# Second attention: each roll's two keys in rows of their own, and one transpose per tile and half

## The chip, the cores and the metric

One core of a Trainium2 chip runs the whole program. The metric is the device time in microseconds, from 3 runs of the kernel before; the profile is of one further execution. The engines are PE (TensorE; its weight loads are listed as PEld), DVE (VectorE), ACT (ScalarE), POOL (GpSimd) and SP (the queue that issues the DMAs). An engine works through its own queue in order.

## What is computed

The input is x of 16 sequences of 256 tokens with 128 features. Four blocks follow one another, each on a layer norm of x and added to x: a causal attention with 16 heads of 64, a slot FFN, a second attention, and the slot FFN again. The second attention is what matters here:

```python
N, S, D = x.shape; H = 16; hd = D // H            # 16, 256, 128; hd = 8
q = (x @ Wq.T).reshape(N, S, H, hd).transpose(0, 2, 1, 3)
k = (x @ Wk.T).reshape(N, S, H, hd).transpose(0, 2, 1, 3)
v = (x @ Wv.T).reshape(N, S, H, hd).transpose(0, 2, 1, 3)
att = jnp.einsum('nqhd,nkhd->nhqk', q, k)         # q and k run over the 16 heads
att = jax.nn.softmax(att / jnp.sqrt(jnp.asarray(hd, x.dtype)), axis=3)
out = jnp.einsum('nhqk,nkhd->nqhd', att, v).reshape(N, S, D)
return out @ Wo.T + bo
```

After the transpose the second axis is the head, so for every token there are 16 x 16 scores between the heads of that same token, a softmax over them, and a weighted sum of the token's 16 value vectors. The last reshape mixes tokens and heads, which the kernel does by a round trip through DRAM.

## The kernel before

**Order.** The four blocks run one after the other. The second attention works through 16 batches, one sequence of 256 tokens (QT = 2 tiles of 128) each. b_steps writes out by hand the order of the steps of one batch; two batches (par 0 and 1) make one trip of a loop, and run_plan gives the same list to every engine, which picks the steps that concern it. While batch b does its softmax and weighting, the same list holds the rolls, dot products and flips of batch b + 1, and the norm, xt and qk of batch b + 2. "v", "turn", "xt", "qk", "yt" and "project" take turns in two PSUM banks R.

**Scores of one batch.** Queries and keys lie with the feature (head, element) on the 128 partitions and the token along the row: b_qt in f32, the keys as a high and a low f16 part, b_kh and b_kl. For each shift n of 0 to 15 the key of head (h + n) mod 16 is needed beside the query of head h. A "roll" step j does two shifts, 2j and 2j + 1: PE multiplies a permutation matrix by the keys (lines 695 and 697, four f16 matmuls of 256 columns) into one of two banks T (T[j % 2]), after the product two rolls ago has read that bank, and DVE multiplies it by the queries (line 811) into b_prod. There are 8 rolls, 0 to 7. After rolls 0 to 3 comes "dots" 0, after 4 to 7 "dots" 1: four f32 matmuls (line 704) sum the 8 elements of each head by the 0/1 matrix heads; that of roll 4j + n writes partitions 32n to 32n + 15 of bank M[j] (heads has 32 columns, of which the last 16 are zero), 512 columns wide: 256 tokens of the roll's first shift, then 256 of its second. ACT copies the bank to b_st (line 770). "flip" j then turns tokens onto the partitions: per tile t and shift parity e one f32 matmul (line 713) with 128 tokens of b_st as the stationary operand and 64 picked columns of the identity as the moving one, into O, the scores laid out as (tile, shift, head).

**What follows.** "soft": DVE takes the row maximum (line 817, waits for both flips), "shift": PE subtracts it in the bank (line 686), ACT takes the exponential (line 773), DVE sums and inverts it (820, 822). "weigh" 0 and 1: POOL multiplies values and exponentials (line 858), "gather" 0 and 1: DVE sums these over the shifts (line 826). "normal": POOL divides (847), SP stores b_o to DRAM and loads b_y back (1225, 1230); "yt" and "project": PE transposes b_y (722) and applies the output matrix (727 to 736); "add": ACT (780). For the batch ahead: "norm" on DVE and POOL (356, 360, 364, 365), "apply" on ACT (759), "xt": PE transposes (670), ACT and DVE split into xh and xl (751, 800), "qk": PE, then ACT and DVE make b_kh, b_kl and b_qt (753, 803, 755).

**Order on PE within one batch**: v, early (roll 0), shift, roll 1, yt, roll 2, project, roll 3, roll 4, dots 0, roll 5, roll 6, flip 0, roll 7, xt, dots 1, qk, flip 1. On DVE: soft, norm, products 0 and 1, gather 1, products 2 and 3, sumexp, products 4, 5, 6 and 7, xl, gather 0, b_kl.

Of the kernel before, what the change touches and what calls it, by code (L numbers as in the profile page):

```python
# [22 lines left out]
ACT = mybir.ActivationFunctionType  # L23
# [3 lines left out]
NB, SEQ, D = 16, 256, 128  # L27
NT = NB * SEQ // 128
QT = SEQ // 128
H = 16  # L30
# [196 lines left out]
def build(nc, x_in, w_in, shapes, scratch, out):  # L227
    ctx = ExitStack()
    with ctx:
# [85 lines left out]
        b_qt = sb("b_qt", [128, 2, SEQ])  # L315
        b_kh, b_kl = sb("b_kh", [128, 2, SEQ], F16), sb("b_kl", [128, 2, SEQ], F16)
        b_prod = sb("b_prod", [128, ROLLS, 2, SEQ])
        b_st = sb("b_st", [128, 2, 2 * SEQ])
        b_v = sb("b_v", [128, 2, QT, EB, 2 * H])
        b_e = sb("b_e", [128, 2, QT, H, H])  # L320
        b_nm, b_rs = sb("b_nm", [128, QT, H], BF16), sb("b_rs", [128, 2, QT, H])
# [336 lines left out]
        def b_tensor(pe):  # L658
            def do(step, i, fill):
# [40 lines left out]
                elif kind == "dots":  # L700
                    pe.wait_ge(b_multiplied, ROLLS * (b + 1) + 4 * j + 4)
                    wait(pe, b_raised, 2 * b + j + 1)
                    for n in range(4):
                        ins = pe.matmul(M[j][32 * n:32 * n + 32, :], w["heads"][:, :],  # L704
                                        b_prod[:, 4 * j + n, :, :].rearrange("p e t -> p (e t)"), start=True, stop=True)
                    ins.then_inc(b_dotted, 1)
                elif kind == "flip":
                    pe.wait_ge(b_raised, 2 * (b + 1) + j + 1)
                    if j == 0:
                        wait(pe, b_exped, b)  # L710
                    for t in range(QT):
                        for e in range(2):
                            ins = pe.matmul(O[nx][:, t * 256 + 128 * j:t * 256 + 128 * j + 128]  # L713
                                            .rearrange("p (n e h) -> p n e h", n=4, e=2)[:, :, e, :],
                                            b_st[:, j, e * SEQ + t * 128:e * SEQ + t * 128 + 128],
                                            ident[:, :].rearrange("p (n h) -> p n h", n=4)[:, :, 0:H],
                                            start=j == 0 and t == 0 and e == 0, stop=False, skip_group_check=True)
                    ins.then_inc(b_flipped, 1)
                elif kind == "yt":
                    pe.wait_ge(b_loaded, 16 * (b - 1))  # L720
# [20 lines left out]
        def b_scalar(act):  # L741
            bank = [None]

            def do(step, i, fill):
# [17 lines left out]
                elif kind == "v":  # L762
                    wait(act, b_weighed, 2 * b)
                    for n in range(2):
                        ins = act.activation(b_v[:, 1 - par, :, :, n * H:(n + 1) * H],
                                             src[:, 0:SEQ].rearrange("p (t h e) -> p t e h", t=QT, h=H), ACT.Copy)
                    ins.then_inc(b_values, 1)
                elif kind == "dots":
                    act.wait_ge(b_dotted, 2 * (b + 1) + j + 1)
                    act.activation(b_st[:, j, :], M[j][:, :], ACT.Copy).then_inc(b_raised, 1)  # L770
                elif kind == "shift":
                    act.wait_ge(b_shifted, b + 1)
                    act.activation(b_e[:, par, :, :, :], O[par][:, :].rearrange("p (t s h) -> p t h s", t=QT, s=H),  # L773
                                   ACT.Exp, scale=EB ** -0.5).then_inc(b_exped, 1)
                elif kind == "project":
                    bank[0] = R[fill.bank], fill.count
                elif kind == "add":
                    projected, count = bank[0]
                    act.wait_ge(b_filled, count)
                    act.activation(X[:, bass.ds((b - 2) * QT, QT), :], projected[:, 0:SEQ]  # L780
                                   .rearrange("p (t d) -> p t d", t=QT), ACT.Copy).then_inc(b_added, 1)
                elif kind == "yt":
                    act.activation(b_yt[:, :], src[:, 0:SEQ], ACT.Copy).then_inc(b_turned, 1)
# [512 lines left out]
def constants():  # L1296
# [9 lines left out]
    for n in range(H):  # L1306
        for h in range(H):
            for e in range(EB):
                roll[EB * ((h + n) % H) + e, n, EB * h + e] = 1.0
    heads = np.repeat(np.eye(H, 32, dtype=np.float32), EB, axis=0)  # L1310
    onehot = np.zeros((128, 2, 128), np.float32)
    for pair in range(2):
        onehot[[pair, 64 + pair], pair, :] = 1.0
# [65 lines left out]
```

## Time and profile before

| | before |
|---|---|
| runs, median (lowest to highest) | 974.3 us (974.05 to 974.79) |
| profiled execution | 972.47 us |
| its span, first to last instruction | 970.7 us |
| mean granted TensorE clock | 0.929 |
| busy: PE / DVE / ACT / POOL | 82% / 70% / 49% / 42% of the span |
| second attention | from about 631 to 872 us of the span |

Times within the trace are us from the start of the span. Busy times are sums over instructions; a matmul's time is that from its start to its modelled end, so neighbouring matmuls overlap and their busy times don't add up to time in the queue. "x8" is the number of instructions merged into a row, and the time is then that from the start of the first to the end of the last. In brackets stands how long the engine was idle before, and whose end released it.

### The profile page before, as it was taken

To read this page: it belongs to the slowest core of one execution; us is meant where nothing else is said; L and a number is where in the kernel's file an instruction comes from. 1 tells how busy PE (TensorE), PEld (TensorE's weight loads), DVE (VectorE), ACT (ScalarE), POOL (GpSimd) and SP (SyncE) were. 2 spreads that over 40 slices of the span, in tenths; PEclk is the share of its full clock that TensorE was granted. 3 is DMA by queue.
4 is the path that set the end of the run, shared out by engine and by line. 5 is a ranking of instruction groups with operands and counts; after the bars stand their busy time and mean duration, and the time that the engine had idled before them with its cause. 6 is when DMAs were issued, how large, how long until landed. Compare 5 with 4: busy or idle time off the path is not lost.

```text
span 970.7 us, 25469 instructions
## 1 busy us (share of the span) xinstructions
PE 799.1 (82%) x10228; PEld 614.3 (63%) x10228; DVE 682.4 (70%) x1560; ACT 472.6 (49%) x801; POOL 408.9 (42%) x302
## 2 busy tenths in 40 slices
PE   2899999999999999999995876668888888839655
PEld 1687777877788777877774453534555555525434
DVE  4677666676666766676664776548999999967763
ACT  1667666676666766776661423023333433315220
POOL 1445444444455444454442100018877778851000
PEclk9999999999999999999997977679999999957786
DMA  6000000000000000000000000000111111120002
GB/s 264 2 3 1 0 0 0 0 0 0 0 0 0 0 0 0 0 0 0 1 2 2 1 0 1 1 1 11 17 18 20 22 22 18 20 27 1 1 1 87
DMA packets 71586, 13.17 MB, mean 14 GB/s; under 512 B 66432, under 2 KB 70528, under 8 KB 70912
## 3 DMA queue, kind: packets, MB, share of 16 engines
q1 hardware_dynamic: 71552, 12.71, 6.0%
q8 instruction: 23, 0.38, 0.2%
q14 instruction: 11, 0.09, 0.0%
HBM read 8.51 MB, written 4.19 MB: 13 GB/s over the span
## 4 chain that ended last, share of the span: by engine, by line
PE 67%; DVE 19%; issue 6%; ACT 5%; POOL 3%; DMA 1%; DVEq 0%; SPq 0%; ACTq 0%; POOLq 0%
PE PS L525 6%; PE PS L482 6%; PE PS L341 6%; PE PS L342 5%; PE PS L343 5%; PE PS L418 4%; DVE b_prod L811 4%; PE PS L704 3%; PE PS L518 3%; PE PS L713 3%; PE PS L504 3%; PE PS L508 2%; PE PS L506 2%; PE PS L695 2%; PE PS L489 2%
## 5 line engine op out<-in xcount | busy, mean ns | idle before, releaser
L626 POOL TENSOR_TENSOR a_pl<-a_p,a_ph 128x1024 f16<-128x1024 f32 (+1 forms) x128 | 210.4, 1644 | 273.5 <-ACT a_ph L551 273.5
L858 POOL TENSOR_TENSOR b_w<-b_v,b_e 128x2048 f32<-128x2048 f32 x32 | 137.7, 4306 | 6.8 <-ACT b_e L773 6.8
L548 ACT ACTIVATE a_p<-PS 128x1024 f32<-128x1024 f32 (+1 forms) x128 | 103.8, 811 | 75.6 <-PE PS L489 75.5
L593 DVE TENSOR_REDUCE a_nm<-PS 128x4 bf16<-128x512 f32 (+1 forms) x128 | 121.3, 947 | 0.0
L541 ACT ACTIVATE a_qk_h<-PS 128x512 f16<-128x512 f32 x128 | 73.3, 604 | 79.5 <-PE PS L343 78.6
L551 ACT ACTIVATE a_ph<-PS 128x1024 f16<-128x1024 f32 (+1 forms) x128 | 103.0, 804 | 0.0
L811 DVE TENSOR_TENSOR b_prod<-PS,b_qt 128x512 f32<-128x512 f32 x128 | 83.0, 678 | 15.8 <-PE PS L697 15.0
L341 PE MATMUL PS<-xh,a_wqk_h 128*128 128x256 f16 x256 | 70.8, 277 | 27.1 <-DVE xl L577 26.9
L582 DVE TENSOR_TENSOR a_qk_l<-PS,a_qk_h 128x512 f16<-128x512 f32 x128 | 87.0, 681 | 2.8 <-ACT a_qk_h L541 2.8
L364 POOL TENSOR_TENSOR veps<-mv,eps 128x2 f32<-128x2 f32 (+2 forms) x40 | 7.9, 198 | 189.4 <-DVE mv L1132 137.1
L695 PE MATMUL PS<-b_kh,w_rolls 128*128 128x256 f16 x256 | 64.7, 281 | 20.6 <-DVE b_prod L811 19.7
L504 PE MATMUL PS<-a_vh,a_ph 128*128 128x65 f16 x768 | 78.5, 196 | 0.5 <-issue 0.5
L506 PE MATMUL PS<-a_vl,a_ph 128*128 128x64 f16 x768 | 78.3, 194 | 0.0
L508 PE MATMUL PS<-a_vh,a_pl 128*128 128x65 f16 x768 | 78.0, 194 | 0.0
L504 PEld LDWEIGHTS PS<-a_vh,a_ph 128*128 128x128 f16 x768 | 70.5, 98 | 11.2 <-issue 9.6
L826 DVE TENSOR_REDUCE b_s<-b_w 128x128 f32<-128x2048 f32 x32 | 72.8, 2276 | 4.9 <-POOL b_w L858 4.9
L589 DVE TENSOR_TENSOR a_vl<-PS,a_vh 128x512 f16<-128x512 f32 x64 | 44.3, 692 | 42.2 <-ACT a_vh L544 42.2
L508 PEld LDWEIGHTS PS<-a_vh,a_pl 128*128 128x128 f16 x768 | 71.4, 98 | 0.0
L506 PEld LDWEIGHTS PS<-a_vl,a_ph 128*128 128x128 f16 x768 | 71.4, 100 | 0.1
L343 PE MATMUL PS<-xh,a_wqk_l 128*128 128x256 f16 x256 | 70.4, 275 | 0.0
L342 PE MATMUL PS<-xl,a_wqk_h 128*128 128x256 f16 x256 | 70.3, 275 | 0.0
L697 PE MATMUL PS<-b_kl,w_rolls 128*128 128x256 f16 x256 | 64.2, 278 | 0.0
(220 smaller groups left out, 2060.7 us busy)
## 6 DMA issues: line engine op xcount, KB each, us to landing
scratch_dram<-b_o SPq DMA_DIRECT2D x32, 64.0 KB, 3.5
b_y<-scratch_dram SPq DMA_DIRECT2D x16, 128.0 KB, 2.1
out_dram<-X SPq DMA_DIRECT2D x2, 1024.0 KB, 3.9
w_rest<-rest_dram SPq DMA_DIRECT2D x1, 1846.0 KB, 14.6
X<-x_dram SPq DMA_DIRECT2D x1, 1792.0 KB, 10.7
w_first<-first_dram SPq DMA_DIRECT2D x1, 1600.0 KB, 6.6
w_rolls<-rolls_dram SPq DMA_DIRECT2D x1, 512.0 KB, 15.2
X<-x_dram SPq DMA_DIRECT2D x1, 256.0 KB, 3.1
```

Of the source, the lines that this page charges most:

```text
L341: pe.matmul(dst, ah, bh, start=start, stop=False, skip_group_check=True)
L342: pe.matmul(dst, ah, bl, start=False, stop=False, skip_group_check=True)
L343: return pe.matmul(dst, al, bh, start=False, stop=stop, skip_group_check=True)
L504: pe.matmul(O[q][:, h * W:(h + 1) * W], ph[:, nx, par, pair, at], a_vh[:, (g - 1) % GA, k, h, :], start=first, stop=False, skip_group_chec ...
L506: pe.matmul(O[q][:, h * W:h * W + EA], ph[:, nx, par, pair, at], a_vl[:, (g - 1) % GA, k, h, :], start=False, stop=False, skip_group_check ...
L508: ins = pe.matmul(O[q][:, h * W:(h + 1) * W], pl[:, nx, par, pair, at], a_vh[:, (g - 1) % GA, k, h, :], start=False, stop=h == 3 and k == ...
L548: act.activation((a_p0, a_p1)[j][:, me, :, :, :].rearrange("p a h q -> p a (h q)"), TT[:, :, 0:512 - 256 * j], ACT.Exp, scale=EA ** -0.5)
L551: act.activation((a_ph0, a_ph1)[j][:, me, :, :, :].rearrange("p a h q -> p a (h q)"), TT[:, :, 0:512 - 256 * j], ACT.Exp, scale=EA ** -0.5 ...
L593: dve.tensor_reduce(a_nm[:, nx, j, :].rearrange("p (a h) -> p a h", a=2)[:, :, 0:2], MM[:, :, 0:256 * (j + 1)].rearrange("p a (h k) -> p a ...
L626: pool.tensor_tensor(*(n[:, g % 2, :, :, :].rearrange("p a h q -> p (a h q)") for n in (pl, p, ph)), ALU.subtract).then_inc(a_split, 1)
L811: dve.tensor_tensor(b_prod[:, j, :, :], T[j % 2][:, :].rearrange("p (e t) -> p e t", e=2), b_qt[:, 1 - par, :].unsqueeze(1).to_broadcast([ ...
L858: pool.tensor_tensor(b_w8[:, j, :, :, :], rolled_values(par, j, 0, H), rolled_exps(par, j, 0, H), ALU.mult).then_inc(b_weighed, 1)
```

## The change

The two shifts of a roll no longer stand side by side along the row of M but in partitions of their own. The matrix heads becomes two of them, [128, 2, 32]: the first writes its sums to columns 0 to 15 of a block of 32, the second to columns 16 to 31. A dots step is eight f32 matmuls of 256 columns in place of four of 512; the one of the second shift accumulates onto the one of the first. What M and b_st hold is half as wide (256 columns), with all 128 partitions holding scores. A flip is then one transposing f32 matmul of 128 columns per tile, two in place of four matmuls, and O has the same layout as before. The semaphores and the order of the steps stay.

```diff
--- before.py
+++ after.py
@@ -315,7 +315,7 @@
         b_qt = sb("b_qt", [128, 2, SEQ])
         b_kh, b_kl = sb("b_kh", [128, 2, SEQ], F16), sb("b_kl", [128, 2, SEQ], F16)
         b_prod = sb("b_prod", [128, ROLLS, 2, SEQ])
-        b_st = sb("b_st", [128, 2, 2 * SEQ])
+        b_st = sb("b_st", [128, 2, SEQ])
         b_v = sb("b_v", [128, 2, QT, EB, 2 * H])
         b_e = sb("b_e", [128, 2, QT, H, H])
         b_nm, b_rs = sb("b_nm", [128, QT, H], BF16), sb("b_rs", [128, 2, QT, H])
@@ -700,21 +700,19 @@
                 elif kind == "dots":
                     pe.wait_ge(b_multiplied, ROLLS * (b + 1) + 4 * j + 4)
                     wait(pe, b_raised, 2 * b + j + 1)
-                    for n in range(4):
-                        ins = pe.matmul(M[j][32 * n:32 * n + 32, :], w["heads"][:, :],
-                                        b_prod[:, 4 * j + n, :, :].rearrange("p e t -> p (e t)"), start=True, stop=True)
+                    for e in range(2):
+                        for n in range(4):
+                            ins = pe.matmul(M[j][32 * n:32 * n + 32, 0:SEQ], w["heads"][:, e, :], b_prod[:, 4 * j + n, e, :],
+                                            start=e == 0, stop=e == 1)
                     ins.then_inc(b_dotted, 1)
                 elif kind == "flip":
                     pe.wait_ge(b_raised, 2 * (b + 1) + j + 1)
                     if j == 0:
                         wait(pe, b_exped, b)
                     for t in range(QT):
-                        for e in range(2):
-                            ins = pe.matmul(O[nx][:, t * 256 + 128 * j:t * 256 + 128 * j + 128]
-                                            .rearrange("p (n e h) -> p n e h", n=4, e=2)[:, :, e, :],
-                                            b_st[:, j, e * SEQ + t * 128:e * SEQ + t * 128 + 128],
-                                            ident[:, :].rearrange("p (n h) -> p n h", n=4)[:, :, 0:H],
-                                            start=j == 0 and t == 0 and e == 0, stop=False, skip_group_check=True)
+                        ins = pe.matmul(O[nx][:, t * 256 + 128 * j:t * 256 + 128 * j + 128], b_st[:, j, t * 128:(t + 1) * 128],
+                                        ident[:, :], is_transpose=True, start=j == 0 and t == 0, stop=False,
+                                        skip_group_check=True)
                     ins.then_inc(b_flipped, 1)
                 elif kind == "yt":
                     pe.wait_ge(b_loaded, 16 * (b - 1))
@@ -767,7 +765,7 @@
                     ins.then_inc(b_values, 1)
                 elif kind == "dots":
                     act.wait_ge(b_dotted, 2 * (b + 1) + j + 1)
-                    act.activation(b_st[:, j, :], M[j][:, :], ACT.Copy).then_inc(b_raised, 1)
+                    act.activation(b_st[:, j, :], M[j][:, 0:SEQ], ACT.Copy).then_inc(b_raised, 1)
                 elif kind == "shift":
                     act.wait_ge(b_shifted, b + 1)
                     act.activation(b_e[:, par, :, :, :], O[par][:, :].rearrange("p (t s h) -> p t h s", t=QT, s=H),
@@ -1307,7 +1305,7 @@
         for h in range(H):
             for e in range(EB):
                 roll[EB * ((h + n) % H) + e, n, EB * h + e] = 1.0
-    heads = np.repeat(np.eye(H, 32, dtype=np.float32), EB, axis=0)
+    heads = np.stack([np.repeat(np.eye(H, 32, n * H, dtype=np.float32), EB, axis=0) for n in range(2)], axis=1)
     onehot = np.zeros((128, 2, 128), np.float32)
     for pair in range(2):
         onehot[[pair, 64 + pair], pair, :] = 1.0
```

## Rows read from the trace of the kernel before

**Rows 1.** The page: busy us, share of the span and instructions of each engine.

```profile
PE 799.1 (82%) x10228; PEld 614.3 (63%) x10228; DVE 682.4 (70%) x1560; ACT 472.6 (49%) x801; POOL 408.9 (42%) x302
```

**Rows 2.** Busy time by stretch: PE, PEld, DVE, ACT, POOL; granted clock, DMA share, GB/s.

```profile
664.50:678.80 14.30, 11.12 (x84) 6.13 (x81) 12.26 (x21) 4.50 (x11) 10.56 (x8) 0.88 0.17 19
...
745.20:758.50 13.30, 11.45 (x96) 7.23 (x93) 12.38 (x21) 5.13 (x13) 10.38 (x7) 1.00 0.17 20
```

**Rows 3.** Waits of DVE, 678.8 to 838.2: us in total, times, longest.

```profile
DVE b_prod L811 <- PE PS L697: 8.3, 24, 0.5
DVE b_nm L817 <- PE PS L713: 1.0, 6, 0.2
```

**Rows 4.** Groups by shape, 678.8 to 838.2: busy us, mean ns | idle before, releaser.

```profile
L704 PE MATMUL PS<-b_prod,w_rest 128*32 128x512 f32 x192 | 25.6, 604 | 7.6 <-DVE b_prod L811 7.2
...
L770 ACT ACTIVATE b_st<-PS 128x512 f32<-128x512 f32 x24 | 14.3, 597 | 57.0 <-PE PS L704 57.0
...
L751 ACT ACTIVATE xh<-PS 128x256 f16<-128x256 f32 x12 | 4.6, 384 | 19.5 <-PE PS L670 19.5
...
L670 PE MATMUL PS<-w_first,xn 128*128 128x128 f32 x24 | 4.6, 272 | 0.0
```

**Rows 5.** Timeline of one steady batch: start, length, engine, line, operation.

```profile
752.20 0.63 DVE L811 TENSOR_TENSOR b_prod<-PS,b_qt 128x512 f32<-128x512 f32 x1
...
752.88 0.28 PE L695 MATMUL PS<-b_kh,w_rolls 128*128 128x256 f16 x1
...
753.00 1.29 DVE L811 TENSOR_TENSOR b_prod<-PS,b_qt 128x512 f32<-128x512 f32 x2 [0.18 <-PE PS L697]
...
753.22 0.27 PE L697 MATMUL PS<-b_kl,w_rolls 128*128 128x256 f16 x1
753.22 0.97 PEld L713 LDWEIGHTS PS<-w_first,b_st 128*128 128x128 f32 x8
...
754.80 0.69 DVE L811 TENSOR_TENSOR b_prod<-PS,b_qt 128x512 f32<-128x512 f32 x1 [0.52 <-PE PS L697]
...
755.55 1.07 PE L704 MATMUL PS<-b_prod,w_rest 128*32 128x512 f32 x8 [0.56 <-DVE b_prod L811]
755.78 2.28 DVE L826 TENSOR_REDUCE b_s<-b_w 128x128 f32<-128x2048 f32 x1
...
757.41 0.38 ACT L753 ACTIVATE b_kh<-PS 128x256 f16<-128x256 f32 x1
...
757.98 0.41 DVE L803 TENSOR_TENSOR b_kl<-PS,b_kh 128x256 f16<-128x256 f32 x1
...
758.48 0.69 DVE L817 TENSOR_REDUCE b_nm<-PS 128x32 bf16<-128x512 f32 x1
```

**Rows 6.** Timeline of the batch before that one.

```profile
739.77 1.29 DVE L811 TENSOR_TENSOR b_prod<-PS,b_qt 128x512 f32<-128x512 f32 x2 [0.26 <-PE PS L697]
...
741.49 0.69 DVE L811 TENSOR_TENSOR b_prod<-PS,b_qt 128x512 f32<-128x512 f32 x1 [0.43 <-PE PS L697]
...
745.23 0.69 DVE L817 TENSOR_REDUCE b_nm<-PS 128x32 bf16<-128x512 f32 x1 [0.16 <-PE PS L713]
```

**Rows 7.** Timeline of the prologue: both flips, then the transposes of xt.

```profile
648.18 2.00 PE L713 MATMUL PS<-w_first,b_st 128*128 128x64 f32 x16
...
650.33 0.41 PE L670 MATMUL PS<-w_first,xn 128*128 128x128 f32 x2 [0.15 <-ACT xn L759]
```

**Rows 8.** Timeline of PE in the second FFN: f32 matmuls in two column halves.

```profile
903.09 3.71 PE L908 MATMUL PS<-f_xs,f_al 128*64 128x129 f32 x32 [3.56 <-DVE f_al L1070]
```

**Rows 9.** Timeline at the end of the last batch with rolls ahead.

```profile
851.05 0.69 DVE L817 TENSOR_REDUCE b_nm<-PS 128x32 bf16<-128x512 f32 x1 [0.79 <-PE PS L713]
```

**Rows 10.** Busy time by stretch, columns as in Rows 2: three short stretches.

```profile
748.00:751.40 3.40, 2.47 (x22) 1.66 (x25) 3.40 (x4) 0.88 (x2) 3.40 (x2) 1.00 0.00 0
666.00:669.40 3.40, 1.27 (x9) 0.62 (x8) 3.40 (x4) 1.14 (x3) 3.24 (x5) 1.00 0.00 0
669.40:672.80 3.40, 2.93 (x13) 0.73 (x14) 2.50 (x5) 0.00 (x0) 3.40 (x3) 0.50 0.02 5
```

## The prediction

> **What bounds the kernel now.** The page comes first [rows 1]: PE is busy 82% of the span and DVE 70%, but these are averages over stages, and the change touches only the second attention (functions b_*). So the next view is the table of busy time by stretch, one stretch per batch [rows 2]. A steady batch lasts 13.30 us; in it DVE is busy 12.38 us, PE 11.45, POOL 10.38 and ACT 5.13, and the granted clock is 1.00. DVE is the engine nearest to full, and PE's busy time is that of overlapping matmuls. What matters is then what DVE still waits for. The table of waits over the twelve steady batches from 678.8 to 838.2 us has only two entries for it, both on PE [rows 3]: 8.3 us before the products of rolled keys (line 811, 24 times, two per batch) and 1.0 us before the row maximum (line 817). That is what any work on PE or ACT can win here; everything else is DVE's own work.
>
> The timeline of one batch tells which PE work ends those waits [rows 5]. In the batch that ends at 758.5 us the product of roll 5 starts at 753.00, the next follows at once, and roll 7's product starts only at 754.80, after 0.52 us idle. PE's queue explains it: after roll 6 stands flip 0, eight weight loads of b_st from 753.22 on (0.97 us), and roll 7 is queued behind it. At the end of the batch the maximum starts at 758.48, some 0.09 us after b_kl was done at 757.98 + 0.41; flip 1 is what came last. In the batch before, the same two waits are 0.43 and 0.16 us [rows 6]. So a flip is on the path twice per batch, each time for less than its own length.
>
> **Flips: eight records become two.** Before, a flip is four f32 matmuls of 64 columns, which run as eight load and matmul pairs, each pair 0.11 to 0.12 us after the last one (0.97 us for the eight loads) [rows 5]. After, it is two transposing f32 matmuls of 128 columns. The kernel has this very form in xt: 24 such records, 272 ns each [rows 4], and a pair of them covers 0.41 us at most [rows 7], so the second starts about 0.11 to 0.14 us after the first and each is one record. I take 2 x 0.11 = 0.22 us of PE's queue where 8 x 0.11 = 0.9 stood: 0.67 us less per flip.
>
> **Flip 0, on roll 7.** Roll 7 cannot use all 0.67 us. It writes the bank that roll 5's product reads, so it must wait for that product. The lag is visible one roll earlier [rows 5]: product 4 ends at 752.20 + 0.63 = 752.83, PE starts roll 6 at 752.88, its last matmul ends at 753.22 + 0.27 = 753.49. That is 0.66 us from the end of a product to a filled bank, and DVE starts 0.04 later (0.70). Product 5 ends near 753.69, so product 7 can start at 754.39 instead of 754.80: **0.41 us**. In the other kind of batch it starts at 739.77 + 0.69 + 0.70 = 741.16 instead of 741.49 [rows 6]: 0.33 us. What is late next is the ping-pong of two banks itself, about 0.1 us. Even a transpose that ran as two passes (0.44 us) would end at 753.66, before roll 7 may start.
>
> **ACT's copy and flip 1, on the maximum.** The copy b_st falls from 128x512 (597 ns) to 128x256, for which the row of xh has 384 ns [rows 4]: 0.21 us less. Flip 1 ends 0.67 + 0.21 = 0.88 us earlier relative to the dot products, and DVE has b_kl to do until then, so the wait before the maximum goes. DVE's instructions that need nothing start about 0.08 us before the former one's end (755.78 + 2.28 = 758.06 against 757.98 [rows 5]), so going from 0.09 idle to back to back is worth **0.17 us**, and 0.24 in the other kind. Both kinds then gain 0.57 to 0.58 us. Late next is b_kl: it follows the sum of line 826 on DVE and needs b_kh from ACT, which ends at 757.41 + 0.38 = 757.79, against a start at 757.98. About 0.15 us of cover is left there.
>
> **Dot products: the same columns in twice the passes.** Before, four matmuls of 512 columns in four column groups, two records each, 1.07 us in all [rows 5]; one record takes 604 ns [rows 4], so the second set of four starts about 0.45 us after the first. After, eight matmuls of 256 columns, accumulating in pairs: sixteen records, four sets of four. Each column group still streams 4 x 256 = 2 x 512 columns. Below, the bound is 0. Above, if each added set paid the latency that a lone record has over its streaming (604 - 427 ns, 427 being 512 columns at the two cycles of 2.4 GHz that 0.45 us amounts to), 2 x 0.18 = 0.36 us per dots step. The nearest row is line 908, f32 matmuls of 129 columns that alternate between two column halves and accumulate: 32 records, sixteen sets of two, in 3.71 us [rows 8], 0.23 us a set at half clock, where 129 columns at two cycles of 1.2 GHz are 0.215. So sets follow with hardly a gap. I take 0.025 us for each added set, **0.05 us per dots step**. For dots 0 roll 5 is queued behind it and DVE waits for roll 5 already, so all of it is lost; for dots 1 the 0.15 us at b_kh cover it, or at worst 0.03 is lost. The stationary blocks add 16 KB to a load at the very start, 600 us before their use; I cost that at nothing.
>
> **Other queues.** No wait is added and no step moves, on SP and POOL neither. POOL is busy 10.38 of 13.30 us [rows 2] and starts each round from DVE's statistics, so it follows. The yt transposes wait for a load whose time hangs on POOL; behind yt on PE stands roll 2, which waits for product 0 anyway.
>
> **The sum.** A steady batch gains 0.57 - 0.05 - 0.02 = 0.50 us; twelve of them 6.0. The first two batches with rolls ahead gain as much, 1.0. In the last one DVE has no b_kl, and it waits 0.79 us for flip 1 [rows 9]. The product of roll 7 comes 0.41 earlier and flip 1 then another 0.88 minus 0.05, and the sum of line 826 (2.28 us) is what remains before the maximum: 1.1 us, which goes on through POOL to the end of the stage. In the prologue both flips end before the transposes of xt, which wait for xn [rows 7]: nothing, and 0.05 lost at dots 0. Together 6.0 + 1.0 + 1.1 - 0.1 = **8.0 us**. The profiled execution took 972.47 us (span 970.7 plus 1.8 around it) and would be 964.5, its span 962.7; the median of the runs is 1.8 us above it, so the forecast is 974.3 - 8.0 = **966.3 us**.
>
> **Rival 1: the clock (slower).** The loop runs at 2.4 GHz because PE keeps working. In the batch from 664.5 on, PE was busy 1.27 of 3.40 us, and then the clock stood at 0.50 (1.2 GHz) for 669.4 to 672.8 [rows 10]; that batch took 14.30 us, 1.0 more than a steady one [rows 2]. The change takes matmuls away and puts transposes in. If every batch got one such stretch, 15 x 1.0 - 8.0 = +7 us: 981 us; it decides against the change from eight stretches on. Against it: the least busy part of a steady batch (748.0 to 751.4, PE 2.47 of 3.40 us [rows 10]) holds neither flip nor dots and is not touched, and the flips lie between rolls and products of the projections. Chance 7%. The Trainium skill speaks for this rival (TensorE: Matmul & The Clock Gate, Part 4: PE-mode transpose): it says that transposes don't count as PE activity for the gate. By that rule, where it decided, this rival's 981 us would be the time and not 966.3; the trace has four transposes in every steady batch at clock 1.00, but no stretch with eight.
>
> **Rival 2: longer dot products take the place of the flips.** If an added set costs 0.09 us and not 0.025, dots 0 gives 0.18 back at roll 5, and dots 1 0.1 through b_kh: 0.29 us a batch, 4.6 us in all, 969.7 us, chance 10%. At the upper bound of 0.36 per dots step nothing is left (0.57 - 0.36 - 0.2): about 974 us, 4%. Against it speaks the row of line 908.
>
> **Rival 3: more than forecast.** If the waits at rolls 5 and 7 closed altogether (another 0.3 us per batch, say because sets of 256 columns leave PE sooner), the gain is 8.0 + 15 x 0.3 = 12.5 us: 961.8 us. Against it: the lag of 0.70 us between products two apart, which the change doesn't touch. Chance 6%.
>
> **How the numbers follow.** The forecast's own case has 73% and spans 963 to 969.5: that allows a slow stretch more or fewer in this stage or in the second FFN behind it, which starts 8 us earlier (each about 1 us), and 0.1 us per batch in either sum. With the 4.6 us case and most of rival 3 the range is 962 to 971. About 0.2%, 1.9 us, is what a measurement of this kernel can tell from no change. Faster by more: 73 + 10 + 6 = 89%; within it 4%; slower 7%.
>
> **What would show it.** In the changed profile: flips as two records each, 64 in all; b_st at about 384 ns; DVE's wait before line 817 gone; of the waits before line 811 the one at roll 7 down to about 0.1 us and the one at roll 5 at 0.2 to 0.3; a steady batch of 12.8 us; the eight records of a dots step now sixteen, in 1.05 to 1.15 us; clock 1.00 in the loop. The prediction is wrong if the dots step is longer than 1.3 us, if the clock drops within the loop, or if b_kl starts to wait for ACT.

## The result, and the profile after

The changed kernel takes 968.86 us (median of 13 runs, 962.97 to 970.79); the kernel before, run beside it on the same chip, 975.39 us (13 runs, 974.05 to 977.52). The ratio is 0.9925, with a 95% interval of 0.991 to 0.994: 0.75% faster. The forecast was 966.3 us with 962 to 971 around it, and a gain of 8.0 us; the measured gain is 6.5 (as a time the kernel is 2.6 us above the forecast, 1.1 of which is that the kernel before, too, took 975.4 and not 974.3 in this group). The size is nearly right, but the gain isn't made up as forecast: one part is larger, and one price wasn't in the sum. The two profiled executions show less of it: 970.23 us after, 1.4 above its median, and 972.47 before, 2.9 below its own, which makes 2.2 us.

The page first, of the kernel after (busy us, share of the span, instructions):

```profile
span 968.4 us, 25597 instructions
...
PE 790.5 (82%) x10292; PEld 604.0 (62%) x10292; DVE 681.9 (70%) x1560; ACT 464.7 (48%) x801; POOL 408.7 (42%) x302
```

Against [rows 1] PE has 64 records more: each of the 32 dots steps has eight more, each of the 32 flips six fewer. Its busy time fell by 8.6 us, and ACT's by 7.9. DVE's own work is the same to 0.5 us, so the span can only have fallen through DVE's waits.

Next, the span cut in three at the first and the last row maximum of the rolls (line 817 before, 815 after): what lies ahead of the batches, the loop over them, and what follows. First before, then after; the columns are those of [rows 2]:

```profile
0.00:653.40 653.40, 558.01 (x8472) 459.25 (x8472) 424.13 (x983) 369.91 (x582) 236.80 (x190) 0.95 0.03 10
653.40:851.00 197.60, 167.51 (x1327) 104.16 (x1327) 181.85 (x293) 74.03 (x172) 153.69 (x100) 0.99 0.16 19
851.00:970.70 119.70, 73.55 (x430) 50.88 (x429) 76.45 (x286) 28.66 (x47) 18.42 (x12) 0.73 0.08 23
```

```profile
0.00:655.70 655.70, 559.00 (x8476) 458.71 (x8476) 424.22 (x983) 369.45 (x582) 236.78 (x190) 0.95 0.03 10
655.70:846.50 190.80, 154.64 (x1387) 93.27 (x1387) 181.07 (x293) 66.49 (x172) 153.51 (x100) 0.98 0.17 19
846.50:968.40 121.90, 76.90 (x429) 52.06 (x429) 76.61 (x287) 28.75 (x47) 18.43 (x12) 0.69 0.09 23
```

The loop is 6.8 us shorter, and both parts outside it are 2 us longer. In them is work that the change hardly touches, and the profiles of the kernels below that have no third store show them vary from one to the next: 652.8 to 655.7 us ahead, 118.3 to 122.5 behind. The part behind is longer where its mean clock is lower (0.69 here, 0.73 before). So a single profile tells of the change only in its middle row, and the medians carry 2 or 3 us of the rest.

Within the loop, two stretches of one batch each:

```profile
745.90:758.60 12.70, 10.58 (x95) 6.26 (x95) 12.31 (x22) 4.60 (x12) 10.36 (x7) 1.00 0.18 21
...
691.40:707.40 16.00, 12.99 (x95) 8.12 (x95) 12.53 (x22) 4.49 (x12) 10.34 (x7) 0.79 0.18 26
```

The ten steady batches from 707.64 to 834.93 take (834.93 - 707.64) / 10 = 12.73 us each, against 13.28 before (13.25 and 13.32 in turn). But one batch, from 691.4 on, takes 16.0 us at a mean clock of 0.79. That is the part that the forecast doesn't have.

What DVE waits for in the ten steady batches after (us in total, times, longest), the answer to [rows 3], and the groups that answer to [rows 4]:

```profile
DVE b_prod L809 <- PE PS L697: 2.2, 10, 0.3
```

```profile
L705 PE MATMUL PS<-b_prod,w_rest 128*32 128x256 f32 x320 | 21.4, 385 | 6.4 <-DVE b_prod L809 6.0
...
L768 ACT ACTIVATE b_st<-PS 128x256 f32<-128x256 f32 x20 | 7.7, 383 | 47.6 <-PE PS L705 47.6
...
L713 PE MATMUL PS<-w_first,b_st 128*128 128x128 f32 x40 | 7.6, 273 | 0.0
```

The wait before the maximum is gone, and the 8.3 us in twelve batches before the products are 2.2 in ten. The timeline of the batch that answers to [rows 5] shows what is left:

```profile
751.98 1.07 PE L705 MATMUL PS<-b_prod,w_rest 128*32 128x256 f32 x16
...
753.63 2.09 DVE L809 TENSOR_TENSOR b_prod<-PS,b_qt 128x512 f32<-128x512 f32 x3 [0.18 <-PE PS L697]
...
753.95 0.38 PE L713 MATMUL PS<-w_first,b_st 128*128 128x128 f32 x2
...
758.20 0.42 DVE L801 TENSOR_TENSOR b_kl<-PS,b_kh 128x256 f16<-128x256 f32 x1
...
758.57 0.69 DVE L815 TENSOR_REDUCE b_nm<-PS 128x32 bf16<-128x512 f32 x1
```

The products of rolls 5, 6 and 7 are now one group of three. Roll 5 still waits 0.18 us, as in [rows 5], and roll 7 about 0.1, too short for the view to show as a wait (three back to back would take 1.9 us and not 2.09: its product starts 0.1 after the one ahead has ended, and not 0.08 before). The flip is two records in 0.38 us. Sixteen records of dots take 1.07 us, which is what eight took. The maximum starts at 758.57, 0.05 before b_kl's 758.20 + 0.42: back to back.

### The profile page after: what moved, and what is told of

Same layout as the page of the kernel before. It is cut to its first block, busy times and chain, and to the rows that moved or that the text cites. A ratio compares the mean times of both kernels' runs of the same rounds, so it can differ in the third digit from the quotient of the medians.

```text
span 968.4 us, 25597 instructions
## 1 busy us (share of the span) xinstructions
PE 790.5 (82%) x10292; PEld 604.0 (62%) x10292; DVE 681.9 (70%) x1560; ACT 464.7 (48%) x801; POOL 408.7 (42%) x302
## 4 chain that ended last, share of the span: by engine, by line
PE 63%; DVE 20%; issue 6%; ACT 5%; POOL 4%; DMA 2%; DVEq 0%; SPq 0%; ACTq 0%; POOLq 0%
PE PS L525 6%; PE PS L482 6%; PE PS L341 6%; PE PS L342 4%; PE PS L343 4%; PE PS L418 4%; DVE b_s L824 3%; PE PS L518 3%; PE PS L504 3%; DVE b_prod L809 3%; PE PS L508 2%; PE PS L506 2%; PE PS L695 2%; PE PS L489 2%; PE PS L461 2%
```

## The batch of 16 us

Its timeline (start, length, engine, SPq being SP's DMA issues), kernel after:

```profile
686.63 3.03 SPq L1223 DMA_DIRECT2D scratch_dram<-b_o  x2
...
691.65 0.68 DVE L815 TENSOR_REDUCE b_nm<-PS 128x32 bf16<-128x512 f32 x1
...
692.98 0.36 SPq L1228 DMA_DIRECT2D b_y<-scratch_dram  x1
...
695.03 0.69 PE L720 MATMUL PS<-w_first,b_y 128*128 128x128 f32 x2 [1.82 <-DMA b_y<-scratch_dram]
...
699.36 1.31 SPq L1223 DMA_DIRECT2D scratch_dram<-b_o  x2
...
700.01 0.69 DVE L809 TENSOR_TENSOR b_prod<-PS,b_qt 128x512 f32<-128x512 f32 x1 [2.70 <-PE PS L697]
...
703.84 0.36 SPq L1228 DMA_DIRECT2D b_y<-scratch_dram  x1
```

SP issues the two stores of b_o, waits until both have landed, and then issues the load of b_y, which lands some 2.0 us later. One batch later, at 699.36, the pair takes 1.31 us and the load follows 4.48 us behind the first store's issue. Here the pair takes 3.03 us and the load follows after 6.35. The load is 1.9 us late, PE stands idle 1.82 us at yt, and behind yt stand roll 2 and all the rest of the batch.

For comparison, PE's yt in a steady batch of the kernel before:

```profile
746.64 0.38 PE L722 MATMUL PS<-w_first,b_y 128*128 128x128 f32 x2
```

Its load was issued at 744.11 and landed at 746.20, some 0.45 us before PE came to yt; in the steady batches of that profile this margin is 0.3 to 0.5 us. In the kernel after, yt starts 0.04 us behind the landing in every steady batch: nothing is left of it.

In the long batch two things happen, which the stretches show:

```profile
690.70:694.10 3.40, 2.01 (x18) 1.19 (x16) 3.33 (x10) 1.92 (x5) 1.11 (x4) 1.00 0.19 18
694.10:697.50 3.40, 2.47 (x10) 1.47 (x11) 3.11 (x3) 1.15 (x3) 3.32 (x3) 0.57 0.12 35
697.50:701.00 3.50, 3.50 (x20) 2.61 (x23) 0.99 (x2) 0.00 (x0) 3.50 (x3) 0.50 0.16 11
```

PE was busy 2.01 of 3.40 us, and right behind, the clock falls to 0.50 (1.2 GHz) until 701.0; DVE, busy 0.99 of 3.50 us, waits 2.70 for roll 3. What the idle time costs without the fall of the clock is seen below, in the run with the dots loops exchanged: 0.8 us of the 3.2.

So there are two theories of what the change did to the loop. **Theory 1**: less work on the path brings PE to yt sooner, so that the load of b_y, which hangs on POOL and the DMAs, has lost its margin; one late store then costs 3 us or more. (A margin of 0.4 us would not have covered a load that is 1.9 us late either; it would have made the idle time shorter.) **Theory 2**: eight transposing matmuls a batch keep the engine less active than ordinary ones, and this is what the clock fell for. And the 16 us batch could be an accident that has nothing to do with either; a long batch stands in the profile before too ([rows 2], 14.30 us).

## The experiments

**The changed kernel once more**, unchanged, beside the others of its group.

> The changed kernel itself, beside the others of this group. Its steady batch should again be 12.73 us and the second attention some 8 us shorter than before where no slow stretch falls into it; the theory of a lost margin (the load of b_y now lands after PE reaches yt) expects some runs with a batch lengthened by 1 to 3 us, and a spread of several us between runs, where the kernel before spreads over 1 to 3.

Measured: 968.03 us (6 runs), 0.9936 (0.9921 to 0.9952) of the kernel before, which took 974.34 in this group. In the profile the same batch takes 15.89 us, again with a load 6.07 us behind its stores, and the others 12.7. The long batch is no accident of one execution; the loop takes 190.7 us. The wider spread that was expected isn't there in this group: 967.21 to 969.91 us, the kernel before 971.82 to 976.29.

**yt later, in the kernel after.** Only the written order on PE (and the order of DVE's steps with it) is changed: yt and what it feeds go behind roll 2, and the projection behind roll 3.

```diff
     put(one, ("roll", 0), ("roll", 1))
-    put(before, "yt")
     put(former, ("gather", 1))
-    put(two, "apply")
...
     put(one, ("roll", 2))
-    put(before, "project")
+    put(before, "yt")
+    put(two, "apply")
     put(one, ("roll", 3))
+    put(before, "project")
```

> The changed kernel with yt after roll 2 and the project step after roll 3, so that PE reaches yt about 1.3 us later than the load of b_y lands. Theory 1 (a late DMA round trip stops PE at yt, and the clock falls behind it): the wait for b_y goes, no slow stretch in steady batches, 965 to 967 us and a spread near that of the kernel before. Theory 2 (fewer and transposing matmuls by themselves let the clock fall): no change against the changed kernel, 966 to 970.

Measured: 961.25 us (6 runs), 0.9876 (0.9850 to 0.9902). The same late pair of stores is there, 6.29 us ahead of the load, and it costs hardly anything:

```profile
684.68 2.98 SPq L1223 DMA_DIRECT2D scratch_dram<-b_o  x2
...
689.71 0.68 DVE L815 TENSOR_REDUCE b_nm<-PS 128x32 bf16<-128x512 f32 x1
...
690.97 0.36 SPq L1228 DMA_DIRECT2D b_y<-scratch_dram  x1
...
693.09 0.44 PE L720 MATMUL PS<-w_first,b_y 128*128 128x128 f32 x2 [0.64 <-DMA b_y<-scratch_dram]
...
702.52 0.69 DVE L815 TENSOR_REDUCE b_nm<-PS 128x32 bf16<-128x512 f32 x1
```

The batch takes 702.52 - 689.71 = 12.81 us, and the whole loop 187.6 at clock 1.00:

```profile
653.80:841.40 187.60, 150.82 (x1387) 92.74 (x1387) 180.88 (x294) 65.23 (x172) 153.74 (x100) 1.00 0.17 19
841.40:959.70 118.30, 71.20 (x429) 48.99 (x429) 76.38 (x287) 28.54 (x47) 18.43 (x12) 0.75 0.09 24
```

The loop wins 190.7 - 187.6 = 3.1 us against the kernel after, which is what theory 1 wants there. But 965 to 967 us was expected, with a narrower spread, and the medians differ by 6.8 us with six runs of 959.39 to 967.66. The two profiles differ by 968.1 - 959.7 = 8.4: 3.1 in the loop, 3.7 behind it and 1.6 ahead of it. More than half of what this run gained is then not explained by yt.

**The same move in the kernel before** tells whether the order is better by itself.

> The kernel before with the same move of yt and project. Both theories: within 1 us of the kernel before, since PE did not wait for b_y in its steady batches; a gain here would mean that the move is worth something by itself and that e2 shows nothing of the change.

Measured: 973.65 us (12 runs), ratio 0.9998 (0.9986 to 1.0009): nothing. Its loop takes 196.6 us against 197.6. The 1.0 is the long batch of 14.3 us, which this profile lacks; two other profiles of kernels built on the one before, with yt in its old place, lack it too (13.11 and 13.36), so it isn't the move's doing. In the loop the move is worth something only in the changed kernel, which is what theory 1 says. The pair of this kernel and the last also gives the change's own worth with the load out of the way: 196.6 - 187.6 = 9.0 us in the loop.

**Flips as ordinary matmuls**: the same operands and columns, without the transposing mode.

```diff
-                                        ident[:, :], is_transpose=True, start=j == 0 and t == 0, stop=False,
+                                        ident[:, :], start=j == 0 and t == 0, stop=False,
```

> The changed kernel with the flips as ordinary f32 matmuls by the identity (two records each, four per flip) in place of transposing ones. By the sum nothing changes in a steady batch (12.73 us), since roll 7 waits for product 5 anyway. Theory 1: same time and same spread as the changed kernel. Theory 2, and the Trainium skill's sentence (TensorE: Matmul & The Clock Gate, Part 4) that transposes don't count as activity: fewer slow stretches and 2 to 4 us less.

Measured: 964.41 us (6 runs), 0.9901 (0.9882 to 0.9920), 3.6 us faster than the kernel after. Taken alone that reads for theory 2: no batch of 16 us, and clock 1.00 over the whole loop of 188.2 us. But in this profile the store wasn't late in the batch in question:

```profile
684.60 1.34 SPq L1223 DMA_DIRECT2D scratch_dram<-b_o  x2
...
689.07 0.36 SPq L1228 DMA_DIRECT2D b_y<-scratch_dram  x1
...
697.34 1.32 SPq L1223 DMA_DIRECT2D scratch_dram<-b_o  x2
...
702.94 0.36 SPq L1228 DMA_DIRECT2D b_y<-scratch_dram  x1
```

1.34 us for the pair and 4.47 to the load; the late load came a batch later, 5.60 us behind its stores, and that batch took 13.01 us. So this run alone leaves theory 2 open.

**Both at once**: yt later and flips as ordinary matmuls. If the mode costs clock, this must beat yt later alone.

> The changed kernel with yt and project moved, and the flips as ordinary f32 matmuls. Theory 1: the same as with yt moved alone, 961 us within 2 us, since PE no longer waits for b_y and the kind of the flip is hidden: the 3.6 us between the changed kernel and its form with ordinary matmuls came from where the late store fell. Theory 2 (transposes lower the clock): again some 3 us less than with yt moved alone, 957 to 959 us.

Measured: 965.14 us (6 runs), 0.9915 (0.9892 to 0.9938), where 961.25 was to be beaten. The loop:

```profile
653.00:840.90 187.90, 155.14 (x1447) 100.76 (x1447) 181.07 (x294) 65.21 (x172) 153.69 (x100) 1.00 0.17 19
```

187.9 us at clock 1.00, against 187.6 at clock 1.00 with transposes. The ordinary flips have four records for two (1447 against 1387 matmuls in the loop) and bring nothing. Theory 2 falls as it was put: eight transposes a batch don't lower the clock by themselves. One form of it isn't tested: that transposes make a fall more likely once PE stands idle at yt. In these two profiles PE idles there 0.64 us at most within the loop, and no kernel with ordinary flips was run with the third store that comes below. The expected 961 us is missed by 4: 0.3 us of it is in the loop, 2.9 in the stretch behind it (121.2 against 118.3), 0.8 less ahead; these are profiles of single executions, and why the medians differ there I can't say.

**Yt later, a second time**, to see whether 961 us holds in another group.

> The kernel with yt and project moved once more. Its second attention should again be 187.6 us from the first to the last row maximum. The forms that came after it (roll 5 first, ordinary matmuls) had attention stages within 1 us of it and yet medians 4 to 5 us above it, with the difference in the second FFN behind the last maximum, 118.3 against 121 to 122 us. If that difference belongs to the kernel, 961 us again; if it is where the clock's slow stretches happen to fall in the stages outside the attention, anything from 960 to 966 us, with the last part between 118 and 122 us.

Measured: 961.33 us (4 runs), 0.9886 (0.9866 to 0.9907), loop 187.5 us. Here no store was late (4.46 to 4.56 us to the load in every batch), and the batch in question took 12.71 us, 0.1 less than with the late store. It holds; the part behind the loop took 118.4 us, as with yt later the first time.

**A third store ahead of the load**, in three kernels, delays every b_y: this doses what theory 1 takes for the cause. The extra store writes rows that nobody reads. (POOL's wait for the stores counts in steps of 48 too, and scratch has four slots in place of two.)

```diff
+                sp.dma_start(scratch[2 + b % 2][:, 0:128, :].rearrange("h p e -> p h e"),
+                             b_o[:, 0, :, :]).then_inc(b_stored, 16)
-                sp.wait_ge(b_stored, 32 * (b + 1))
+                sp.wait_ge(b_stored, 48 * (b + 1))
```

In the kernel after:

> The changed kernel with a third store of b_o per batch (one tile again, to a place of its own), which puts some 1.2 us between the store and the load of b_y in every batch. Theory 1: PE waits at yt for the load, 1.2 us longer in each batch, stands idle there, and the clock falls in many or all steady batches: those grow from 12.73 to 13 to 16 us, the whole by 10 to 40 us. Theory 2 (the kind and number of matmuls sets the clock, the wait at yt is harmless): steady batches stay at 12.73 us, and only the 2 to 3 us at the exposed end are added.

In the kernel before:

> The kernel before with the same third store. It reaches yt about 0.4 us after the load has landed, so 1.2 us leave it 0.8 us of waiting, less than the changed kernel has. Theory 1: fewer slow stretches and a smaller loss than in the changed kernel. Theory 2: 13.28 us per batch as before.

In the kernel after with yt later:

> The changed kernel with yt and project moved later, with the same third store: the 1.3 us of margin take the 1.2 us. Theory 1: steady batches at 12.73 us, clock 1.00, and 2 to 3 us more at the exposed end only. Theory 2: the same as the changed kernel with the third store.

Measured: 978.86 us (8 runs, 1.0065, 1.0042 to 1.0088), 976.94 (8 runs, 1.0027, 1.0003 to 1.0050) and 970.14 (8 runs, 0.9953, 0.9933 to 0.9972). Against the same kernels without it (968.03, 974.53, 961.25; the first and the last from an earlier group) the third store costs 10.8, 2.4 and 8.9 us. The loops alone take 201.5, 199.0 and 194.3 us: 10.7 more than in the kernel after, 1.3 more than in the kernel before (2.4 if its long batch is left out, 199.0 - 196.6), 6.7 more than with yt later. The load now comes 6.0 to 6.1 us behind the first store's issue in nearly every batch, 1.6 later than before. Here is one and the same stretch of the three, the kernel after first, then the kernel before, then yt later:

```profile
668.00:850.00 182.00, 143.10 (x1246) 89.10 (x1247) 163.22 (x259) 59.27 (x155) 139.90 (x90) 0.94 0.24 24
```

```profile
668.00:850.00 182.00, 152.94 (x1219) 96.03 (x1223) 167.56 (x265) 65.67 (x157) 142.24 (x90) 1.00 0.25 25
```

```profile
668.00:850.00 182.00, 145.09 (x1290) 89.11 (x1290) 169.64 (x267) 59.90 (x158) 142.04 (x91) 0.97 0.25 26
```

and what PE waits for the load in it, in the same order:

```profile
PE PS L720 <- DMA b_y<-scratch_dram: 13.5, 8, 2.4
```

```profile
PE PS L722 <- DMA b_y<-scratch_dram: 12.5, 13, 1.5
```

```profile
PE PS L720 <- DMA b_y<-scratch_dram: 7.7, 12, 2.0
```

The kernel before waits nearly as long for the load in sum, but in shorter pieces, and its clock stays at 1.00; it has 13.3 us a batch, and its steady batches become 13.25 to 13.62. The kernel after has batches of 12.7 us and, in between, seven of 13.5 to 15.7: the clock falls in six of them. A delay that is the same for both costs 1 to 2 us of one loop and 11 of the other, as a lost margin would have it. The two kernels differ in the kind of their flips too, so this pair alone doesn't exclude the form of theory 2 that was left above.

That yt later pays 8.9 us was not expected: 2 to 3 was. In twelve of its fifteen batches the move does what it should: 12.7 to 12.8 us (10.67 and 12.52 in the first two) at clock 1.00 from the second batch on, with at most 0.7 us of idle time at yt. The other three make up the loop's 6.7 us. One (15.77) has the late pair of stores on top of the third (7.67 us to the load). The last (13.78) has a load 6.27 us behind and 1.38 us idle at yt. In the third (14.28) the load is no later than in its neighbours and PE idles 0.54 us at yt, and still the clock falls, so idle time at yt isn't all that decides it. One of the falls in the kernel after, in its timeline and in two stretches:

```profile
762.84 0.44 PE L720 MATMUL PS<-w_first,b_y 128*128 128x128 f32 x2 [1.49 <-DMA b_y<-scratch_dram]
...
766.48 0.69 DVE L809 TENSOR_TENSOR b_prod<-PS,b_qt 128x512 f32<-128x512 f32 x1 [1.23 <-PE PS L697]
```

```profile
761.40:764.80 3.40, 1.84 (x13) 1.34 (x14) 3.40 (x4) 1.29 (x4) 3.24 (x5) 1.00 0.13 39
764.80:768.20 3.40, 3.39 (x25) 2.04 (x27) 2.13 (x5) 0.00 (x0) 3.40 (x3) 0.51 0.00 0
```

It is the same course as in the kernel after at 694: PE idles at yt for 1.49 us, the clock falls right behind that stretch (mean 0.51 in the next one), and only then does DVE wait.

**The place of flip 0 instead of its length**, in the kernel before: flip 0 behind roll 7.

```diff
-    put(one, ("roll", 6), ("flip", 0), ("roll", 7))
+    put(one, ("roll", 6), ("roll", 7), ("flip", 0))
```

> The kernel before with flip 0 queued behind roll 7 instead of in front of it, nothing else. The sum gives the wait before roll 7's product 0.41 and 0.33 us per batch to win, which this order frees without any change to flips or dot products; xt then stands behind the flip (1.0 us on PE), but the sum of 2.28 us on DVE doesn't hide it, since xl comes first: that takes the gain back. Expected: product 7 starts 0.4 us earlier, xl 0.5 to 0.6 us later than it could, the batch at 13.2 to 13.5 us, 973 to 977 us. If a steady batch falls below 12.9 us, the shorter flip was not needed for the gain, only its place.

Measured: 977.07 us (10 runs), 1.0031 (1.0010 to 1.0052): slower. The timeline:

```profile
754.96 2.09 DVE L811 TENSOR_TENSOR b_prod<-PS,b_qt 128x512 f32<-128x512 f32 x3 [0.17 <-PE PS L697]
...
757.84 0.42 DVE L800 TENSOR_TENSOR xl<-PS,xh 128x256 f16<-128x256 f32 x1 [0.79 <-ACT xh L751]
```

The products of rolls 5, 6 and 7 stand in one group as they do after the change, so the reading of [rows 5] is right: flip 0 was what held roll 7 back. But the 0.9 us of flip 0 only move on to the transposes of xt behind it, and xl waits 0.79 us (eleven times between 700 and 840 us, 8.7 in all); the batches take 13.50 and 13.59 us in turn. What the change gains is the flip's length, and it can't be had by its place.

**The order of the two loops in a dots step**, in the kernel after: each column group gets its two passes one behind the other, instead of four sets of four.

```diff
-                    for e in range(2):
-                        for n in range(4):
+                    for n in range(4):
+                        for e in range(2):
```

> The changed kernel with the two loops of the dots step exchanged: both shifts of one column group in a row, then the next group. In the trace of the changed kernel the sixteen records take 1.07 us, four column groups at a time. If the groups still run side by side in this order, the step stays near 1.1 us and the batch at 12.73 us. If a record waits for the one before it in its own group, and the others behind it, the step grows towards 16 x 0.21 = 3.4 us: then roll 5 and b_kh come up to 2.3 us later each and the batch is 15 to 17 us.

Measured: 963.13 us (2 runs only), 0.9889 (0.9854 to 0.9925). The step takes as long as before:

```profile
746.74 1.09 PE L705 MATMUL PS<-b_prod,w_rest 128*32 128x256 f32 x16
```

1.09 us against 1.07, a steady batch of 12.77 against 12.73. How the passes are ordered among the column groups doesn't matter here. The median below that of the kernel after isn't from the dots: in this profile the late load (6.01 us behind its stores) cost 0.8 us and not 3.2, and the loop took 188.7 us. It is worth a look, since it parts the idle time from the clock:

```profile
691.97 0.44 PE L720 MATMUL PS<-w_first,b_y 128*128 128x128 f32 x2 [1.62 <-DMA b_y<-scratch_dram]
```

```profile
688.80:702.30 13.50, 10.32 (x95) 6.54 (x95) 12.43 (x21) 4.49 (x12) 10.37 (x7) 1.00 0.19 25
```

PE idles 1.62 us at yt, as long as in the second profile of the kernel after (1.63), but the clock stays at 1.00 and the batch takes 13.5 us, not 15.9. So the idle time costs about 0.8 us and the fall of the clock about 2.4, and idle time of this length doesn't always bring the fall. What tips it was not found. Two runs are too few to say more of the median.

**Roll 5 ahead of dots 0**, on top of yt later, goes for the wait that is left.

```diff
-    put(one, ("roll", 4), ("dots", 0), ("roll", 5))
+    put(one, ("roll", 4), ("roll", 5), ("dots", 0))
```

> The changed kernel with yt and project moved, and roll 5 queued before dots 0. DVE's wait before product 5 (0.18 and 0.26 us per batch) goes, since roll 5 needs only product 3, and dots 0 still ends before roll 6 may start: 12.73 - 0.2 = 12.5 us per batch, 15 x 0.2 = 3 us less than the kernel with yt moved alone, 958 us. If dots 0 with its 1.07 us delays roll 6 instead, the gain is 0 to 0.1 us per batch.

Measured: 966.38 us (6 runs), 0.9919 (0.9895 to 0.9944). 958 was expected, or a gain of at most 0.1 us per batch if dots 0 delayed roll 6. The loop is 186.8 us, 0.8 less than with yt later alone, and the rest is again outside: the part behind it takes 122.5 us at a mean clock of 0.69.

```profile
655.30:842.10 186.80, 151.90 (x1387) 92.64 (x1387) 180.89 (x294) 65.23 (x172) 153.70 (x100) 1.00 0.17 19
```

A batch takes 12.68 us, a gain of 0.05 where 0.2 was hoped for: roll 5 comes on time, and the wait returns as 0.13 and 0.14 us before the products of rolls 6 and 7, where the two banks take turns. So rival 3, which wanted another 0.3 us a batch out of these waits, has next to nothing to take.

The best kernel that was run is the one with yt later: 961.25 and 961.33 us in two groups, 0.988 and 0.989 of the kernel before.

## Why the prediction was right, and where not

- **What bounds the loop**: right. DVE's work stayed the same, and what the batches lost is what DVE had waited.
- **Flip 0 and roll 7**: right. The product of roll 7 waits about 0.1 us (0.43 and 0.52 before), as forecast, and roll 5 keeps 0.18.
- **b_st and flip 1**: right. 383 ns for 384, no wait before the maximum, and b_kl doesn't wait for ACT.
- **Dots**: the price was over-estimated. 0.05 us a step was taken, with 0.36 as the upper bound; measured is 1.07 us before and after, so nothing. That accounts for the 13.28 - 12.73 = 0.55 us that a steady batch gained, where 0.50 was forecast. Rival 2 is out with it, in both orders of the loops.
- **The last batch**: 12.87 against 11.59 us, 1.28 for the 1.1 forecast. The sum over the loop, freed of the late load and of the long batch before, is 9.0 us (6.6 in the twelve steady batches, 1.2 in the first two, 1.3 in the last, each rounded), against the 8.1 that the forecast has within it (6.0 + 1.0 + 1.1).
- **"Other queues"**: this is the step that failed. It said that yt waits for a load whose time hangs on POOL, and that behind yt stands roll 2, "which waits for product 0 anyway", and costed it at nothing. That holds for a load on time: in the stretch from 700 to 840 us after, PE or its weight loads wait for it ten times, 2.5 us in all, and no batch is longer for it. It doesn't hold for a late one. With a batch shorter by 0.55 us, PE is at yt sooner by most of that (the margin of 0.3 to 0.5 us is gone) and the load is not, since the stores and the load keep their 4.47 us. The store that was late by 1.7 us then went past roll 2's cover, and the clock's fall made 3.2 us of it (15.98 - 12.8). So the loop's account is: 9.0 from the shorter batches, 1.0 more because the profile before has a long batch that the one with yt later hasn't (197.6 against 196.6), 3.2 back for the late load: 6.8. The terms are differences between the same few profiles, so that they add up to the 197.6 - 190.8 measured is no test; the 3.2 alone was read from the long batch itself as well. That the medians' gain of 6.5 us lies so near the forecast's 8.0 is in part luck: the sum over the loop was 0.9 too small and lacked the 3.2 of the late load, and the parts outside the loop moved by 2 us each between two profiles.
- **Rival 1, the clock**: it did fall once within the loop, but by another mechanism than the rival's. A clock that drops within the loop was also one of the forecast's own signs of being wrong, and in one batch it came. The rival put it down to the matmuls taken away and the transposes put in; it fell where PE stood idle at yt, and in one batch, where the rival needed eight. The runs speak against the transposes themselves: with yt later, eight a batch stand in a loop of 187.5 us at clock 1.00, and ordinary matmuls in their place give 187.9. The Trainium skill (TensorE: Matmul & The Clock Gate, Part 4: PE-mode transpose) says that transposes don't count as busy for the gate in the way that matmuls do; at eight a batch, no effect of that is seen in these loops, and whether it helps a fall along where PE stands idle isn't tested.
- **The parts outside the loop** were taken as unchanged but for about 1 us. They are 2.3 + 2.2 = 4.5 us longer in the profile after, and 1.0 us shorter in the one with yt later (959.7 - 187.6 = 772.1 against 970.7 - 197.6 = 773.1). What stays open: why the second FFN falls into one course of the clock or another, and why each kernel keeps to one in the median. It decides 5 us in the medians of kernels whose loops are within 1 us of each other (961.3 with yt later, 966.4 with roll 5 ahead of dots 0 on top).
- **Open as well**: what moves a transfer of instructions onto one pair of stores. The load is issued 5.2 to 6.4 us behind the stores in the second round of six profiles without the third store (after, after again, yt later, the exchanged dots loops, and the two built on yt later), one round later with ordinary flips (in both kernels that have them), and nowhere in yt later's second run, nor in the kernel before or those built on it. A transfer of instructions on queue q8 lies in the same stretch in all of them, and its time against the stores tells them apart. Here it is, first in the kernel after (DMA view from 687.6 to 687.8), then in the kernel before (690.6 to 690.8):

```profile
q8 instruction: 1, 0.02, 46.9%
```

```profile
q8 instruction: 1, 0.02, 33.0%
```

In the kernel after it starts at 687.70, 1.1 us behind the first store's issue, in the kernel before at 690.70, 4.2 us behind, when the stores are all but through. In the loops of all profiles without a third store the same holds: where it starts 1.1 to 1.3 us behind the first store, the load is 1.5 to 1.9 us late; at 2.3 to 2.5 us, 1.1 to 1.2; with roll 5 ahead of dots 0, where it starts at the same moment as the store, 0.7; and where it starts 0.4 us or more ahead, or 3.5 us or more behind, at most 0.1. So the late store goes with the transfer and not with the margin, and in the profiles it meets the stores only in kernels built on the changed one. That is read from profiles; no run moved the transfer alone, and what sets its time stays open.

## What to carry to other kernels

When a loop gets shorter, look in every queue for the step that waits for something whose time doesn't shrink with it (a store and a load behind it), and see how much margin it has now and what is queued behind it; put it behind the next step that the critical engine needs. A short idle time of PE can cost more through the clock than by itself (here 2.4 us against 0.8), but it doesn't do so each time. And compare profiles by the part of the span that the change can touch: here the rest varied by more than half of the gain.

## What the chip showed that wasn't expected

- Four f32 matmuls of 512 columns in four column groups, and eight of 256 columns accumulated in pairs, take the same 1.07 us; in the other order of the passes 1.09.
- A transposing f32 matmul of 128 columns is one record (273 ns, two in 0.38 us), an ordinary one of the same operands two records: 1447 matmuls in the loop for 1387.
- Two falls of the clock shown here stand right behind idle time of PE (1.82 us at yt in the kernel after, 1.49 with the third store), and the first makes 3.2 us of a load that was 1.9 late. But 1.62 us idle at the same place, with the dots loops exchanged, brought no fall and cost 0.8, and one fall with yt later and the third store came behind 0.54 us idle at yt.
- Two stores that are issued in 1.31 us in nearly all batches took 2.7 to 3.0 in one, at the same place of the program in four of the profiles, each time with a transfer of 16 KB of instructions that starts 1.1 to 1.3 us behind the first store's issue.
